# Issuing each gather of routed rows in front of the scatter that it used to follow

## The reference

```python
x = x + tanh(g_xattn[0]) * xattn(layernorm(x), ctx_512, ...)   # 16 heads, self + cross (1601 context rows)
h = layernorm(x)
out = shared_expert(h)                       # silu(h @ sg.T) * (h @ su.T) @ sd.T, 704 hidden
scores, idx = top_k(softmax(h @ wr.T + rb), 2)          # 7 routed experts, the best 2 per token
w = per-token weights of the 7 experts (scores normalised, 0 where not chosen)
for e in range(7):
    out = out + w[..., e:e+1] * expert(h, rg[e], ru[e], rd[e])
x = x + tanh(g_ffn[0]) * out
```

## Time and profile before

| | us |
|---|---|
| median of 3 runs | 1475.22 |
| the profiled execution | 1474.51 |
| its span, first to last instruction | 1472.8 |
| first start of `up` in turn 1 | 1117.29 |
| first start of `up` in turn 2 | 1125.60 |
| first start of `up` in turn 37, the last | 1451.49 |
| PE busy, share of the span | 94% |
| mean granted TensorE clock | 0.988 |

### The profile page before, as it was taken

The page is one execution under the profiler, slowest core; times in us unless marked ns, Lnnn a source line. Parts: engine busy times, 40 slices in busy tenths (PEclk is TensorE's granted clock), DMA queues, the critical chain, the costliest instruction groups (busy, mean ns, idle before and its releaser), DMA issues.

```text
span 1472.8 us, 27237 instructions
## 1 busy us (share of the span) xinstructions
PE 1386.7 (94%) x7688; PEld 694.5 (47%) x7689; DVE 870.8 (59%) x1804; ACT 728.3 (49%) x1107; POOL 366.1 (25%) x743
## 2 busy tenths in 40 slices
PE   7889899999999999999999999899999999999996
PEld 4445333333333333333333333455566666666664
DVE  6668688888888888888888888265322222222221
ACT  4535577666677666776666777722001222122221
POOL 5455222222222222222222222200001222222222
PEclk9989899999999999999999999999999999999998
DMA  7754211111111111111111110371031111111111
GB/s 237 210 159 156 65 50 48 48 50 46 48 49 48 50 47 50 49 49 49 49 49 49 49 48 34 130 293 71 1 111 32 28 28 28 26 27 28 26 28 26
DMA packets 57711, 98.43 MB, mean 67 GB/s; under 512 B 7441, under 2 KB 42001, under 8 KB 56657
## 3 DMA queue, kind: packets, MB, share of 16 engines
q1 hardware_dynamic: 50384, 88.10, 18.2%
q0 software_dynamic: 7296, 9.97, 4.0%
HBM read 69.20 MB, written 28.58 MB: 66 GB/s over the span
## 4 chain that ended last, share of the span: by engine, by line
PE 69%; DMA 10%; issue 8%; DVE 5%; POOL 5%; ACT 1%; DVEq 0%; POOLq 0%; SPq 0%; ACTq 0%
PE ps L643 18%; PE ps L625 9%; PE ps L525 9%; PE ps L821 7%; DMA wp<-xn_rows,slot_table 7%; PE ps L760 5%; POOL out L1158 4%; PE ps L771 3%; PE ps L692 3%; DMA k_parts<-work 2%; PE ps L539 2%; PE ps L628 2%; PE ps L599 1%; DVE bv L1494 1%; PE ps L798 1%
## 5 line engine op out<-in xcount | busy, mean ns | idle before, releaser
L1213 DVE TENSOR_REDUCE mx<-ps 128x1 f32<-128x512 f32 (+1 forms) x832 | 521.2, 663 | 127.7 <-PE ps L525 97.4
L967 ACT ACTIVATE arena<-ps 128x1024 f32<-128x1024 f32 (+1 forms) x512 | 484.4, 995 | 153.5 <-PE ps L625 149.3
L643 PE MATMUL ps<-arena 128*32 128x512 f32 (+5 forms) x2432 | 290.1, 524 | 0.6 <-ACT arena L967 0.4
L625 PE MATMUL ps<-arena 98*128 98x512 bf16 x832 | 264.4, 381 | 5.1 <-DMA arena<-rowst 5.1
L525 PE MATMUL ps<-arena 96*128 96x512 bf16 x768 | 263.5, 382 | 5.3 <-DVE arena L1278 3.4
L808 PE MATMUL ps<-arena,work 128*128 x608 | 186.4, 460 | 0.6 <-issue 0.6
L1116 POOL TENSOR_SCALAR_AFFINE_SELECT arena<-arena 128x128 f32<-128x128 f32 x256 | 74.8, 292 | 438.3 <-ACT arena L967 428.4
L525 PEld LDWEIGHTS ps<-arena 96*128 96x128 bf16 x768 | 74.2, 97 | 175.3 <-DVE mx L1213 103.2
L1488 DVE TENSOR_TENSOR work<-work,ps 128x352 f32<-128x352 f32 x76 | 39.6, 521 | 179.1 <-ACT work L1033 179.1
L808 PEld LDWEIGHTS ps<-arena,work 128*128 128x128 f32 x608 | 112.5, 190 | 57.4 <-issue 1.1
L1213 DVE TENSOR_REDUCE mneg<-ps 128x2 f32<-128x512 f32 (+2 forms) x192 | 112.5, 640 | 23.4 <-PE ps L535 23.0
(11 more groups left out here) (157 smaller groups left out, 1423.0 us busy)
## 6 DMA issues: line engine op xcount, KB each, us to landing
arena<-in_experts SPq DMA_DIRECT2D x8, 2176.0 KB, 12.1
arena<-k_parts SPq DMA_DIRECT2D x64, 198.1 KB
arena<-k_parts SPq DMA_DIRECT2D x64, 132.1 KB
k_parts<-work SPq DMA_DIRECT2D x24, 300.0 KB, 4.1
q_parts<-work SPq DMA_DIRECT2D x16, 384.0 KB, 3.5
arena<-q_parts SPq DMA_DIRECT2D x64, 96.0 KB
arena<-k_parts SPq DMA_DIRECT2D x64, 66.0 KB
arena<-q_parts SPq DMA_DIRECT2D x64, 64.0 KB
```

The costliest lines, as they stand in the source:

```text
L625: mm = pe.matmul(bk[:, 0:w], kst[r][0:KROWS + MROWS, T + kt * P:T + (kt + 1) * P], qst[r][0:KROWS + MROWS, 1, :], start=True, stop=True)
L643: mm = pe.matmul(ps[32 * q:32 * q + VW, 6, b0:b1], vst[0:kn, r % VR, TT + kt if cross else kt, :], pr[0:kn, c0:c0 + b1 - b0], start=(phase ...
L967: act.activation(pr[:, c0:c0 + n], ps[:, 2 * (g % 2):2 * (g % 2) + 2, :].rearrange("p b n -> p (b n)")[:, 0:n], ACT.Exp, scale=SCALE).then ...
L1213: return dve.tensor_reduce(m, out, AX_X, ALU.max)
```

## The change

One more gather is issued ahead of the loop, and in the loop the gather of tile i+3 stands in front of scatter i, where that of tile i+2 stood. The order on Pool's queue was g0 g1 g2 s0 g3 s1 g4 s2 ...; it becomes g0 g1 g2 g3 s0 g4 s1 g5 s2 ... (g for gather, s for scatter). So each gather from g3 on moves up past one scatter. The number of buffers, all waits, and all other engines' programs stay as they are.

```diff
             pool.wait_ge(S["routed"], 1)
             gather(0)
             gather(1)
+            gather(2)
             for i in range(NSLOT):
-                if i + 2 < NSLOT:
-                    gather(i + 2)
+                if i + 3 < NSLOT:
+                    gather(i + 3)
                 scatter(i)
```

## The result

The changed kernel takes 1436.5 us (median of 4 runs, 1436.2 to 1437.22), the kernel before 1475.26 us (median of 4, 1474.6 to 1477.49): a ratio of 0.9736, 95% interval 0.9724 to 0.9748. That is 38.8 us less. The profiled execution took 1437.22 us with a span of 1435.5.

What follows compares the result with a forecast made beforehand. TensorE was taken to wait each turn for a gather queued behind a scatter on Pool; 35 turns x 8.21 = 287.4 us instead of 325.9 takes the execution from 1474.51 to 1436.0, plus 0.71 for the median: 1436.7 us, range 1434.2 to 1447.5.

Steps and rivals of the forecast that it cites:

- the length of a turn: Routed stage, from one `up` on TensorE to the next: 4.74 + 3.47 = 8.21 us without the wait, 9.311 before.
- visible idle of 27.9 us: TensorE's 35 standstills at the transposes of gathered rows, 0.80 us each; winning back only these would give 1447.3 us.
- turns 13 and 14: Stalled turns before the change: the wait costs 0.97 us before the transposes, then 0.21 (odd turn 13) or 0.08 (14).
- a drained stream: On TensorE, a reason given why the wait costs 0.97 and 0.08 us, more than 0.80 us of visible idle.
- When the gather lands, and its slack: Pool's gather lands 5.6 us into a turn, now for the next turn's transposes: about 7.3 us slack, before 0.9 late.
- The gather's wait holds no scatter: On Pool's queue, the gather's wait for its buffer ends nearly a turn before scatter(i)'s wait for its result; cost nothing.
- TensorE's stream bounds next: Without the gather wait, TensorE's own stream bounds the routed stage, at 8.21 us a turn.
- the loop's jump: On TensorE's queue after `turn_hidden`, with the expert number's load: ready at about 7.2 of 8.21 us, covered by 1.0.
- only part comes back: Rival: jump, register loads and weight loads show in the routed stage, some 0.3 us a turn; 1447.3 us, chance 0.09.
- nothing: Rival: something else that ends with the gather holds TensorE, turns stay at 9.31 us; 1475.2 us, chance 0.03.
- The clock: Rival: TensorE without pauses in the routed stage falls to a granted clock of 0.85; 1487.4 us, chance 0.04.
- The limiter: Peak-current rule for dense matmuls, 13 of 16 clock pulses: kernel 1503.0 us; said never to trip with one busy core.

Runs made afterwards that it cites:

- half experiment: Gathers of tiles 3 to 20 issued in front of the scatter, those of tiles 21 to 37 behind it; 1453.68 us, ratio 0.9864 to the kernel before.
- last delay: Changed kernel with three memsets of 128x2048 float32 on Pool in front of each gather from tile 4 on; 1448.63 us, ratio 0.9831 to the kernel before.
- six places: Changed kernel, but the gather of tile i+6 instead of i+3 stands in front of scatter i; 1435.05 us, ratio 0.9736 to the kernel before.
- seven places: Changed kernel, but the gather of tile i+7 instead of i+3 stands in front of scatter i; 1709.14 us, ratio 1.1592 to the kernel before.

## Why the prediction was right

**The view that carried it.** The prediction took the length of a turn from turn 1 of the trace before, which did not wait, and not from the idle time. 8.21 us was forecast and 8.209 came out; for the 35 turns 287.4 us was forecast and 287.31 measured. The visible idle of 27.9 us would have said 1447.3. That the whole time also came within 0.2 us (1436.7 forecast, 1436.5 measured) is luck: the stage began 1.31 us later than before in the profiled execution, and the median lay 0.72 us below that execution, where the prediction had put it 0.71 above. The half experiment shows the difference at one place: 17 stalls with 13.4 us of visible idle cost 18.5 us. The last delay shows it more sharply, with 14.4 us lost for 4.0 us of visible idle. Turn 7 there, which shows no idle, is 0.23 us longer in front of the transposes (4.96 us) and 0.20 us longer behind them (3.67 us). So the cost beyond the idle has a part on each side of the wait, as the prediction read in turns 13 and 14. The reasons that it gave (a drained stream, and the transposes' weight load behind the wait) are argued from rows; no run takes the two apart, and none shows why odd and even turns differ.

**When the gather lands, and its slack.** Right, and in size too: with a delay of 5.52 us g4 still landed 1.8 us early, so the slack was 7.3 us. What gives out first under a lasting delay is Pool's own time. There the prediction had one term too small: it had 5.3 us to spare from 2.88 us of issuing a turn, and the last delay shows 8.70 - 5.52 = 3.18 us, because the 0.30 us in front of the next scatter was left out. So 5.0 us is the delay that the order can bear turn after turn.

**The gather's wait holds no scatter.** Right: s0 follows its result as before, at 1127.80 - 1118.60 = 9.20 us after the start of turn 1, and 1126.50 - 1117.29 = 9.21 before. g3 came at 1116.87, which is the forecast 1115.5 with the later start of the stage. Where that cover is gone the scatter does slip, as the two runs further forward show: with six places the slip costs nothing, with seven the loop closes.

**TensorE's stream bounds next.** Right: it is busy in all 287.31 us, and the loop's jump, the one thing that turn 1 does not hold, comes in every second turn and adds nothing that shows: turns are 8.20 or 8.21 us.

**Rivals.** That only part comes back, or nothing, is ruled out by the turns of 8.209 us. The clock stayed at 1.00 in the stage with TensorE busy all the time. In the experiment with seven places it fell behind idle time and not in dense work, where the rival looked for it. The Trainium skill, "TensorE: Matmul & The Clock Gate", Part 1, says that the default state is throttled and activity releases the throttle; this case's stretches at 0.53 after idle and 1.00 in dense work agree. The limiter of the same Part 1, which the prediction puts at "a third of its cores", is stated there for a third core of a die that starts dense matmuls, not for a third of them; with one core busy no run here shows it.

**What it did not see.** The stage began 1.31 us later in the profiled execution than before, so that this one took 1437.22 us where 1436.0 was forecast. The code ahead of it is the same. Over the ten profiles turn 1 began anywhere from 1114.61 to 1118.60 us; the granted clock between 50 and 100 us was 0.86 in the changed kernel's profile against 0.93 before, but the kernel with six places had 0.86 there as well and began at 1115.99, so the clock in that stretch alone is not the cause. It stays open, and it means that differences of up to 4 us between single profiles say nothing of this stage.

No version beat the changed kernel: where the order was good, every one had the same 8.21 us a turn, and their medians (1433.72 to 1436.06) differ by less than the runs ahead of the stage do.

## What to carry to other kernels

On an engine that issues in order, a load that feeds the bound engine should not stand behind a store that waits for a late result: count not only the wait but what the store itself puts in front of the load (here 2.4 us, of which 1.88 us from the store's start on). To price such a wait, look in the same trace for a round that did not have it (a first or last one), and take the whole round's length; the idle time alone was 28% too small here (27.9 of 38.6 us), and with the longest delay it was 4.0 of 14.4 us. A load can be moved forward only as far as the buffer it waits for is freed well ahead of what stands behind it; the place where that ends can be a cliff, from nothing at six places to 19% above that at seven (ratios 0.9736 and 1.1592).

## What the runs showed of the hardware

The price of a long wait of TensorE was more than the wait: after 6.33 us without a matmul, the next 12 matmuls took 5.17 us instead of 2.76, at a granted clock of 0.53. The waits of 0.8 us in the kernel before cost no clock (1.00 over the 35 turns). Short waits can be there without idle time in TensorE's records: with the longest delay, turn 7 had none and was 8.63 us long instead of 8.21. A gather started 0.27 us after the result that it was held to, a scatter 0.81 us after it. On GpSimd, an instruction's record need not end before the next one's begins: a memset's starts 1.02 us after a scatter's of 1.57 us, and then lasts 1.52 us, where one of the same size in the kernel before took 0.95. What it adds, 0.93 us, can be read only from start to start of the DMAs.
